# Two causal attention stages: all normalisation in their beginning, and products without a reader on TensorE

## The reference

```python
x = L0_attn_x
x = x + _L0_attn_ref(_layernorm(x), ...)   # stage 0
x = x + _L0_ffn_ref(_layernorm(x), ...)    # stage 1: routed feed-forward
x = x + _L1_attn_ref(_layernorm(x), ...)   # stage 2: causal attention, low-rank q and k
x = x + _L1_ffn_ref(_layernorm(x), ...)    # stage 3: feed-forward sorted by expert
x = x + _L2_attn_ref(_layernorm(x), ...)   # stage 4: a block of its own, generated weights
...                                        # stages 5 to 7

def _L1_attn_ref(hidden_states, q_a, q_b, k_a, k_b, v_w, v_b, o_w, o_b):   # 16 heads of 8 channels
    q = _low_rank_proj(hidden_states, q_a, q_b)          # (x a) b per head
    k = _low_rank_proj(hidden_states, k_a, k_b)
    v = (hidden_states @ v_w.T + v_b).reshape(Bc, Tc, H, HD).transpose(0, 2, 1, 3)
    att = jnp.einsum('bhtd,bhsd->bhts', q, k) * scale
    att = jax.nn.softmax(jnp.where(causal, att, jnp.finfo(att.dtype).min), axis=-1)
    y = jnp.einsum('bhts,bhsd->bhtd', att, v).transpose(0, 2, 1, 3).reshape(Bc, Tc, Dc)
    return y @ o_w.T + o_b
```

## Time and profile before

| what | value |
|---|---|
| median of 3 runs | 1698.59 us |
| the profiled execution's own time, its span | 1698.09 us, 1696.4 us |
| busy share of the span: PE, DVE, ACT, POOL | 82%, 62%, 44%, 45% |
| mean granted TensorE clock | 0.887 of full |
| granted clock in 40 slices of 42.4 us, in tenths | 9788689858999796699978999899999999996597 |
| stage 2; stage 4's attention | 329 to 557 us; 650 to 876 us |

### The profile page before, as it was taken

One profiled execution on the slowest core, in us unless ns is written; L12 is line 12 of the kernel. 1 busy time (PEld: TensorE's weight loads), 2 busy tenths in 40 slices (PEclk: granted clock), 3 DMA queues, 4 the chain that ended last, 5 costly groups with the idle time before them and its releaser, 6 DMA issues. The chain is left out here.

```text
span 1696.4 us, 24924 instructions
## 1 busy us (share of the span) xinstructions
PE 1390.6 (82%) x8907; PEld 844.5 (50%) x8907; DVE 1055.8 (62%) x2864; ACT 747.6 (44%) x1168; POOL 761.0 (45%) x833
## 2 busy tenths in 40 slices
PE   4486679879998795899977999799999999985193
PEld 2355556644444562444435777455554545534062
DVE  5865578567885656688833322578778777756112
ACT  3554244326665341566644432455455454430040
POOL 4533345433333546244442442256555455563533
PEclk9788689858999796699978999899999999996597
DMA  2000005100000322000001020000000000003213
GB/s 90 14 8 1 34 1 213 71 14 1 1 1 1 124 64 100 1 1 2 1 1 52 1 100 1 1 1 1 1 1 1 1 1 1 1 1 124 63 52 98
DMA packets 29563, 52.74 MB, mean 31 GB/s; under 512 B 3217, under 2 KB 24593, under 8 KB 27265
## 3 DMA queue, kind: packets, MB, share of 16 engines
q1 hardware_dynamic: 26144, 44.36, 7.4%
q0 software_dynamic: 3296, 6.78, 1.2%
HBM read 29.07 MB, written 21.02 MB: 30 GB/s over the span
## 5 line engine op out<-in xcount | busy, mean ns | idle before, releaser
L2491 DVE CUSTOM_DVE_ANT_0 s_masked_scores<-s_for_max,s_mask_qk 128x128 bf16<-128x128 f32 (+3 forms) x512 | 227.1, 487 | 58.1 <-PE s_for_max L2312 56.2
L2851 POOL TENSOR_TENSOR wbuf<-s_probs 128x1024 f32<-128x1024 f32 x64 | 152.1, 2376 | 206.6 <-ACT s_probs L3010 206.6
L3010 ACT ACTIVATE s_probs<-s_scores 128x1024 f32<-128x1024 f32 x128 | 132.3, 1033 | 201.7 <-PE s_scores L2932 201.7
L2259 POOL TENSOR_SCALAR_AFFINE_SELECT s_probs<-s_probs 128x256 f32<-128x256 f32 x256 | 100.0, 408 | 247.4 <-ACT s_probs L2418 149.9
L3052 DVE TENSOR_REDUCE s_negmax<-s_for_max 128x2 f32<-128x1024 f32 x126 | 152.1, 1208 | 21.2 <-PE s_for_max L2907 21.2
L2312 PE MATMUL s_for_max<-s_k_stack,s_q_stack 32*128 32x128 f32 (+3 forms) x512 | 142.6, 441 | 26.8 <-DVE s_max_wide L2491 17.4
L3059 DVE RECIPROCAL s_recip<-s_pv_and_sums 128x128 f32<-128x128 f32 x128 | 116.7, 934 | 47.1 <-PE s_pv_and_sums L2958 47.1
L2312 PEld LDWEIGHTS s_for_max<-s_k_stack,s_q_stack 32*128 32x128 f32 x512 | 72.4, 205 | 128.6 <-DVE s_max_wide L2491 86.8
L2418 ACT ACTIVATE s_probs<-s_scores 128x1024 f32<-128x1024 f32 x128 | 127.5, 1025 | 14.0 <-PE s_scores L2333 13.7
L2945 PE MATMUL s_pv_and_sums<-s_probs,s_v 128*64 128x512 f32 x512 | 123.9, 605 | 0.9 <-DVE wbuf L3067 0.9
L2347 PE MATMUL s_pv<-s_probs,s_v_and_one 128*32 128x512 f32 (+3 forms) x1024 | 96.9, 474 | 1.5 <-DVE s_o L2510 1.5
(11 more groups left out here) (574 smaller groups left out, 3436.9 us busy)
## 6 DMA issues: line engine op xcount, KB each, us to landing
rows_by_expert<-s_empty_rows SPq DMA_DIRECT2D x8, 1032.0 KB, 10.5
s_w<-extra SPq DMA_DIRECT2D x2, 2048.0 KB, 9.7
wbuf<-w SPq DMA_DIRECT2D x1, 3460.0 KB, 11.1
s_generators<-extra SPq DMA_DIRECT2D x1, 2898.0 KB, 11.2
wbuf<-w SPq DMA_DIRECT2D x1, 2888.0 KB, 10.0
wbuf<-w SPq DMA_DIRECT2D x1, 2124.0 KB, 8.1
dispatched<-s_empty_slots SPq DMA_DIRECT2D x1, 2064.0 KB, 8.5
s_rows<-dispatched SPq DMA_DIRECT2D x8, 258.0 KB, 2.7
```

The source lines that it names most:

```text
L2259: last = nc.gpsimd.affine_select(out=diag, in_=diag, compare_op=ALU.is_ge, fill=0.0, base=0, pattern=[[0, diag.shape[1]], [1, P]], channel ...
L2491: last = nc.vector.tensor_tensor_reduce(out=junk[:, m % 2, at:at + n], in0=p1[m % 2][:, at:at + n], in1=mask[:, S - n:S], scale=1.0, scala ...
L2851: nc.gpsimd.tensor_tensor(added[half], probs[:, g % 2, 2 * half, :, :], probs[:, g % 2, 2 * half + 1, :, :], ALU.add).then_inc(s_added, 1)
L3010: nc.scalar.activation(probs[:, g % 2, j, :, :], p2[:, :, :], ACT.Exp, scale=dh ** -0.5).then_inc(s_exp, 1)
```

## The change

1. A helper issues products of the 128x128 bf16 identity with 512 columns of itself, which nothing reads.
2. Stage 1: two such products ahead of the last down, three ahead of the last transposes, four behind them. Stage 3: 16 behind its last shared product.
3. Stage 2's start: one per eight factor products and more behind them, ahead of waits. Stage 4's start: groups between waits, which TensorE now does one by one (the moments, rstd, `hi`, `xnT` of chunk 0).
4. In both: behind `q` and `k` of quad 0, and one behind each `max` unit that stands ahead of the first `pv`.
5. Normalisation: statistics of chunk 1 ahead of chunk 0's scaling; VectorE scales all chunks, chunk 1 ahead of `q_stack` of quad 0, chunks 2 and 3 behind it; their transposes go to the score banks, not to `odd_jobs`, behind `q`, `k` and the second `max` unit of quad 0; GpSimd makes all low parts in the beginning.
6. GpSimd's memsets of mask and maxima wait until chunk 0 is scaled; its memset of v stands behind the rstd of chunk 3. In stage 4 hs of chunks 2 and 3 is made in single steps between the cuts of different quads; the bias of stage 2 is added in the beginning.

```diff
@@ Shared
+    def spare_products(self, bank, n):
+        for _ in range(n):
+            self.nc.tensor.matmul(bank[:, 0:TPC * P], self.identb[:, :],
+                                  self.identb[:, :].unsqueeze(1).broadcast_to([P, TPC, P]), start=True, stop=True)
@@ routed_ffn, TensorE
                 down(n)
+                if n == total - 2:
+                    sh.spare_products(ps_comb[n % 2], 2)
+            sh.spare_products(ps_comb[0], 3)
             turn_y(B - 1)
+            sh.spare_products(ps_comb[0], 4)
@@ sorted_ffn, TensorE
             shared_down(B - 1)
+            sh.spare_products(ps_t[0], 16)
@@ causal_plan
-    for c in range(1, B):
-        behind(("max", QUADS * c - 2, 3), ("ln", c))
+    plan.insert(plan.index(("q", 0)), ("rows", 1))
+    behind(("q", 0), ("ln", 1))
+    behind(("q_stack", 0), ("rows", 2), ("rows", 3))
+    behind(("k", 0), ("ln", 2))
+    behind(("max", 0, 1), ("ln", 3))
@@ causal_attention
+    turned_in = [None, p2[0][:, 0:S], p2[0][:, S:2 * S], p2[1][:, 0:S]]
@@ GpSimd
-        ln.rstd_of(pool, 0)
+        for c in range(2):
+            ln.rstd_of(pool, c)
+        pool.wait_ge(ln.s_xn, TPC)
         nc.gpsimd.memset(mask[:, :], 0.0).then_inc(s_mask, 1)
...
-        ln.rstd_of(pool, 1)
+        for c in range(2, B):
+            ln.rstd_of(pool, c)
         nc.gpsimd.memset(v32[:, :, :, :, HD8:32], 0.0).then_inc(s_ones, 1)
...
-        ln.scaled_by(nc.gpsimd, pool, 1)
-        add_bias(0)
-        for c in range(2, B):
-            ln.rstd_of(pool, c)
+        if s_hs is None:
+            for c in range(B):
+                add_bias(c)
+        for c in range(1, B):
+            ln.low_part_by(nc.gpsimd, pool, c)
+        if s_hs is not None:
+            for c in range(2):
+                for step in range(1 + TPC):
+                    make_hs(pool, c, step)
+                add_bias(c)
...
-            c = q // QUADS + 1
-            if c < B and q % QUADS == 0:
-                ln.low_part_by(nc.gpsimd, pool, c)
-            if c + 1 < B and q % QUADS == 1:
-                ln.scaled_by(nc.gpsimd, pool, c + 1)
-            if c < B and q % QUADS == 2:
-                add_bias(c)
+                c, step = divmod(q - 1, 2 + TPC)
+                if s_hs is not None and r == 0 and 0 <= c < B - 2:
+                    if step <= TPC:
+                        make_hs(pool, c + 2, step)
+                    else:
+                        add_bias(c + 2)
@@ TensorE
             if n >= 2:
                 pe.wait_ge(s_exp, n - 1)
+            else:
+                pe.wait_ge(ln.ready, 3 + n)
...
             if item[0] in ("q", "k"):
                 project(item)
+                if item[1] == 0:
+                    sh.spare_products(po, 2 - "qk".index(item[0]))
...
                 scores_for_max(*item[1:])
+                if n < first_pv:
+                    sh.spare_products(po, 1)
...
             elif item[0] == "ln":
-                odd_bank(item)
-                ln.turned(pe, item[1], pm)
+                ln.turned(pe, item[1], turned_in[item[1]])
@@ VectorE
+        ln.stats_of(dve, 1)
         ln.scaled(dve, 0)
...
         st.end()
+        ln.stats_of(dve, 2)
         before_vector(dve)
-        ln.stats_of(dve, 1)
         ln.low_part(dve, 0)
-        for c in range(2, B):
-            ln.stats_of(dve, c)
-        dve.wait_ge(s_mask, 2)
-        dve.wait_ge(s_wide, 1)
+        ln.stats_of(dve, 3)
...
+            if item[0] == "rows":
+                ln.scaled(dve, item[1])
@@ factors_tensor (stage 2)
+                if h % 4 == 3:
+                    sh.spare_products(po, 1)
                 if h == 10:
                     ln.turned(pe, 0)
+            sh.spare_products(po, 1)
+            pe.wait_ge(s_whi, 2)
+            sh.spare_products(po, 2)
+            pe.wait_ge(s_wlo, 1)
+            sh.spare_products(po, 2)
@@ first_rows_tensor (stage 4)
+            sh.spare_products(po, 4)
+            pe.wait_ge(ln.s_mv, TPC)
+            sh.spare_products(po, 2)
+            pe.wait_ge(ln.s_rstd, 1)
+            sh.spare_products(po, 3)
             ln.turned(pe, 0)
+            sh.spare_products(po, 2)
+            pe.wait_ge(ln.s_hi, 1)
+            sh.spare_products(po, 2)
+            pe.wait_ge(ln.ready, 1)
+            sh.spare_products(po, 1)
```

40 lines of the change are left out of this document (21 added, 19 removed).

## The result

The changed kernel takes 1733.6 us (median of 4 runs, 1727.6 to 1735.5), the kernel before in the same session 1699.8: a ratio of 1.0197, 95% interval 1.0176 to 1.0219. It is slower by some 34 us, where 1669 was forecast. The profiled execution took 1733.2 us, span 1731.2, mean granted clock 0.883.

A forecast was written before the change was run, and what follows sets the result against it. TensorE at half clock was taken to bound the first quads, later VectorE and TensorE together. Stage 2's -13.9 and stage 4's -15.4 us gave -29.3 from 1698.6: 1669 us, own range 1663 to 1676, 8 in 10 within 1659 to 1683.

The forecast's parts named there:

- The step that failed: First quads of stages 2 and 4: spare products overfill TensorE's waits, clock rises; less(0) to less(3) -9.9 and -10.3 us.
- Price at full clock: Quads ahead of the first PV: 12 spare products, 2.8 us per quad, cost 0 at full clock; 10.37 us holds.
- The rival of the other side: Clock stays half until PV; 36 spare products at 0.43 us cost +7.2 us per stage, about 1709 us; chance 0.05.
- Stage starts: Start of stages 2 and 4 to the low part of chunk 0: -2.5 and -0.8 us.
- Low part to k_stack: Quad 0: VectorE's added scalings collide with GpSimd's memset and bias additions; +4.0 us in stage 2, +2.0 in stage 4.
- Quads of chunks 2 and 3: Later quads without those chunks' rows take 11.58 us for 13.08 and 13.46; -3.0 us in stage 2, -3.8 in stage 4.
- Stages 1 and 3: Spare products behind them, 9 and 16, cost 0 as nothing waits; up to 0.4 us each end if transposes queue.

The follow-up runs named there:

- after: The changed kernel as described, with all its spare products, against the kernel before: 1733.6 us, ratio 1.0197.
- f3: Changed kernel with each of the 36 spare products per causal stage replaced by one of the same size with real fp32r data: 1756.7 us.
- h1: Changed kernel with each of the 36 spare products per causal stage on 32 rows instead of 128, same 512 columns: 1710.8 us.
- f2: Changed kernel with three spare products instead of one behind each score pair ahead of the first PV: 1719.5 us.
- h3: g3 with one spare product behind each of the 36 score pairs ahead of PV: 1692.2 us.
- k1: h3 with two spare products instead of one behind the third to twelfth score pair of quad 0: 1683.7 us, 0.9868 of the kernel before.
- e1: Changed kernel without the 36 spare products per causal stage behind score pairs, those at stage starts kept: 1690.9 us, 0.9954 of the kernel before.
- h2: Changed kernel with each of the 36 spare products per causal stage on 64 columns instead of 512, all 128 rows: 1717.6 us.
- e2: Changed kernel with all 126 spare products left out, the moved normalisation alone: 1690.6 us, 0.9953 of the kernel before.
- g3: e1 with 9 spare products behind the first k product and GpSimd's memset of v held until all row groups are scaled: 1686.6 us, 0.9897 of before.
- f1: Changed kernel with 22 spare products in place of 1 behind the first k product, the 36 behind score pairs kept: 1714.9 us.

## Why the prediction was wrong

**The step that failed:** "They don't fit, so TensorE is then busy without a gap. That is just the state in which the clock rose at 390 to 395, so I expect half clock to end within some 5 us of the first score pair." The clock first fell while TensorE waited for k_stack. Then TensorE was gapless for 55 us, and the clock stayed at half until 3.8 us behind the first PV product. The earlier trace rows hold two changes at 390 at once, no more waits and PV, and I took the first for the cause. The rows had a warning: 4.84 us of 5 busy had not raised the clock, nor had 44 close records. By the Trainium skill ("TensorE: Matmul & The Clock Gate", Why this matters for your kernels) long gaps are what to avoid. The fall in stage 2, in a wait of 3.29 us, agrees; but having no gap did not bring the clock back, for 55 us at 0.50. What work TensorE does counts: one product on 128 rows per pair did not raise it (after, f3), nor one on 32 rows in its place (h1), three on 128 rows did (f2).

- **Price at full clock, "cost 0"**: mis-sized. A held quad takes 11.65 and 13.13 us ahead of PV, not 10.37; less(0) to less(3) 35.1, not 31.7 (h3, k1). The quad had room for 0.23 us of columns, not for the alternation. With the clock held in both stages, k_stack to less(0) at 14.3 and less(0) to less(3) at 35.1, the change would by estimate have given 1733.6 - 2 x (22.4 - 14.3) - 2 x (52.6 - 35.1) = 1682: the step above accounts for some 51 us of the 64 missed, this term for most of the other 13.
- **The rival of the other side** named the mechanism, with a chance of 0.05 and a price of 0.43 less 8.3 us of waits, +7.2 per stage. Measured: 22.4 - 15.5 and 52.6 - 39.4 (e1) = +20 in stage 2, +21 in stage 4. Each product costs 0.59 us at half clock net of the waits (less(0) to less(1)), since 0.37 of alternation comes on top of the columns (h2). 1709 became 1734.
- **Stage starts**: the low part of chunk 0 came 2.2 and 0.9 us earlier (forecast 2.5, 0.8): right in this execution. In stage 2 the figure spreads: in e1, with the same start, it is 1.7. In e2, with no spare product, it is 1.1, and 0.8 in stage 4. So most of it is the normalisation's; what the spare products add is not told apart from the spread.
- **Low part to k_stack**: +3.5 and +1.8 (9.56 and 7.86 for 6.08 and 6.07), forecast +4.0 and +2.0: right, and by the cause named, as g3 shows. The Trainium skill's rule ("SBUF - State Buffer", Who interferes with whom), that these VectorE instructions and GpSimd's exclude each other for a whole instruction, agrees: 6.11 us beside GpSimd's memset and bias additions, 2.13 without them.
- **Quads of chunks 2 and 3**: 11.6 us, right to 0.02; but the last three quads of each stage gave 2.6 and 2.2 us back in this execution, with short falls of the clock in them. In e1 these quads lost 0.3 and 0.1. The cause is open.
- **Stages 1 and 3**: nothing waits for the spare products there, right. Between its first statistics and those of stage 2, stage 1 took 125.3 us before, 122.8 in this execution and 125.2 in e1, which has the same stage 1; stage 3 took 92.8 and 92.7.

So the normalisation's move is worth -8 us (e2), the 36 products per stage +41, and the other spare products nothing that was measured. The forecast of a gain rested on the clock, and the clock did not come.

## What to carry to other kernels

Before filling waits with products to keep the clock, look at what kind of products ran when it rose, not only at how busy TensorE was, and treat an edge at which two things changed as unexplained. Price a filler by start-to-start times among its neighbours: between products on 32 rows, one on 128 rows costs its columns and some 0.3 (full clock) to 0.4 us (half) more. And try the filler in the smallest number that holds the clock in every execution; where it holds only sometimes, it loses more than it wins: over the stretches from k_stack to less(3), a stage that fell took 20 us more than one without fillers (after and e1), one that held 5 us less (h3 and g3).

## What the runs showed of the hardware

- Granted clock at 0.50 for 55 us with TensorE 55.00 us busy: products on 32 rows alternating one for one with 512-column products on 128 rows. With three of these for each it rose 7.5 and 5.3 us behind k_stack (f2).
- The clock fell at 347.5 us, 1.7 us into a wait of TensorE; in f1 it fell 12.8 us behind k_stack with TensorE busy for 12.58 of 12.82 us.
- Products of 512 columns on 32 rows, on different groups of rows, start together: three within 0.01 us (h1). With a 512-column product on 128 rows between two of them, at half clock, it starts 0.72 us behind the first, and the second 0.54 us behind it (after).
- A spare product on 32 rows, 512 columns, between score products on 32 rows lengthens the chain by 0.09 us at half clock; on 128 rows and 64 columns 0.24, on 128 rows and 512 columns 0.59, and the same with real fp32r data 0.77 (22.11 us for 12.83).
- Two stages of one execution with the same products behind the pairs (h3), one at full clock for the whole stretch, one falling 13.6 us behind k_stack: 35.1 and 51.9 us from less(0) to less(3).
